# A two-layer mixture-of-experts kernel: blank slot rows written one expert at a time, pieces of 64 rows, and the short half of the down product on two halves of the array

## The reference, cut to what matters

```python
buf = zeros((E, C, D)).at[se, pos_c].add(where(valid, x[st], 0))      # E=64, C=384, D=256
g = einsum('ecd,efd->ecf', buf, w_gate)                                # F=176
u = einsum('ecd,efd->ecf', buf, w_up)
eo = einsum('ecf,edf->ecd', silu(g) * u, w_down)
gathered = eo[se, pos_c] * (sw * valid)[:, None]
y = zeros_like(x).at[st].add(gathered)
return y + shared_swiglu(hidden_states, sh_gate, sh_up, sh_down)
```

## Time and profile before

| | |
|---|---|
| runs | 615.86, 617.28, 621.86 us; median 617.28 |
| profiled execution | 624.11 us, of which the span is 622.4 us |
| mean granted TensorE clock | 0.937 of full |
| busy | PE 508.2, PEld 364.2, DVE 313.9, ACT 188.1, POOL 330.0 us |
| moved | 146.55 MB, 92394 packets |
| front | 0 to about 267.6 us; then the expert loop to about 596.1 us; then the last adds and the store |

### The profile page before, as it was taken

The page is one execution under the profiler, slowest core; times in us unless marked ns, Lnnn a source line. Parts: engine busy times, 40 slices in busy tenths (PEclk is TensorE's granted clock), DMA queues, the critical chain, the costliest instruction groups (busy, mean ns, idle before and its releaser), DMA issues.

```text
span 622.4 us, 11506 instructions
## 1 busy us (share of the span) xinstructions
PE 508.2 (82%) x2483; PEld 364.2 (59%) x2484; DVE 313.9 (50%) x823; ACT 188.1 (30%) x398; POOL 330.0 (53%) x289
## 2 busy tenths in 40 slices
PE   0797299489899899979999879999789898999920
PEld 0443153253545355558888757788668776889710
DVE  8731164274866862254445526555265544555424
ACT  0111012011221211033444425454255444455410
POOL 8900050572474767603767635655465545656750
PEclk9997689689999999989999979999799999999975
DMA  6999999996794222238999969999699989899779
GB/s 205 365 390 393 358 393 404 392 363 212 239 309 143 110 84 112 101 98 212 234 231 227 238 134 219 229 213 252 148 205 239 249 220 229 196 243 227 146 148 307
DMA packets 92394, 146.55 MB, mean 235 GB/s; under 512 B 10824, under 2 KB 72120, under 8 KB 92280
## 3 DMA queue, kind: packets, MB, share of 16 engines
q1 hardware_dynamic: 61608, 83.30, 42.6%
q0 software_dynamic: 30672, 61.75, 38.5%
HBM read 81.18 MB, written 63.83 MB: 233 GB/s over the span
## 4 chain that ended last, share of the span: by engine, by line
PE 49%; SPq 19%; DMA 10%; issue 10%; DVE 7%; POOL 3%; ACT 1%; POOLq 0%; DVEq 0%
PE bank L1074 21%; PE bank L1095 7%; PE bank L1096 7%; SPq L356 5%; SPq L355 5%; DMA x_g<-in_x 4%; PE bank L1055 4%; POOL slot_rows L491 3%; PE bank L935 2%; DMA wt<-in_wdt 2%; SPq L392 2%; PE bank L885 2%; SPq L363 2%; DVE M L749 1%; PE bank L956 1%
## 5 line engine op out<-in xcount | busy, mean ns | idle before, releaser
L502 POOL DMA_INDIRECT acc<-sil,sids x64 | 99.3, 1552 | 89.2 <-ACT sil L597 57.8
L491 POOL DMA_INDIRECT slot_rows<-ctok,sli x96 | 95.2, 991 | 80.0 <-issue 27.7
L502 POOL DMA_INDIRECT acc<-OH,sids x63 | 97.6, 1549 | 53.6 <-ACT OH L597 19.3
L1074 PE MATMUL bank<-xgT,wb 128*128 128x192 f32 (+9 forms) x384 | 85.2, 375 | 15.1 <-issue 12.8
L1074 PEld LDWEIGHTS bank<-xgT,wb 128*128 128x128 f32 (+1 forms) x384 | 65.6, 198 | 29.2 <-issue 17.0
L1096 PE MATMUL bank<-wt,hh 128*128 128x256 f32 x254 | 75.5, 379 | 0.0
L849 DVE TENSOR_TENSOR hh<-sg,bank 48x384 f32<-48x384 f32 x64 | 35.6, 556 | 74.0 <-ACT sg L586 73.2
L1096 PEld LDWEIGHTS bank<-wt,hh 128*128 128x128 f32 x254 | 48.3, 190 | 6.6
L584 ACT ACTIVATE sg<-bank 128x384 f32<-128x384 f32 x64 | 31.4, 491 | 55.4 <-PE bank L1074 55.1
L597 ACT ACTIVATE sil<-bank,wcol 128x256 f32<-128x256 f32 x64 | 29.7, 474 | 53.1 <-PE bank L1096 51.7
L597 ACT ACTIVATE OH<-bank,wcol 128x256 f32<-128x256 f32 x64 | 29.8, 474 | 51.3 <-PE bank L1096 50.0
(11 more groups left out here) (185 smaller groups left out, 739.1 us busy)
## 6 DMA issues: line engine op xcount, KB each, us to landing
cw<-slot_rows SPq DMA_DIRECT2D x127, 136.0 KB
cw<-in_cW SPq DMA_DIRECT2D x64, 256.0 KB, 6.2
wb<-in_wblk SPq DMA_DIRECT2D x32, 496.0 KB, 4.1
slot_rows<-xgT POOLq DMA_DIRECT2D x12, 1088.0 KB, 15.9
slot_rows<-wb POOLq DMA_DIRECT2D x12, 1088.0 KB, 25.0
h0T<-in_wblk SPq DMA_DIRECT2D x16, 496.0 KB
hT<-in_wblk SPq DMA_DIRECT2D x16, 496.0 KB
acc<-zrow POOLq DMA_DIRECT2D x2, 2432.0 KB
```

The lines of the kernel that those rows point to most:

```text
L491: pool.indirect_dma_start(slots_d, bass.IndirectOffsetOnAxis(sli[:, g % 2, k, t:t + 1], 0), ctok[:, g % 2, t, :], None, bounds_check=SLOTS ...
L502: pool.indirect_dma_start(acc[u % 2], bass.IndirectOffsetOnAxis(sids[:, u % SR, j:j + 1], 0), yo[u % UE][:, j, :], None, compute_op=ALU.ad ...
L1074: ins = mm(bank[o][0:m, 0:n], w(b, c), xgT[u % UE][:, c, 0:n], start=c == 0, stop=c == DC - 1)
```

## The change

1. **Blank rows.** The table is laid out expert by expert, 448 rows each (384 and 64 spare). POOL's 24 transfers, `s_init` and the two VectorE operations per group that made block numbers go. VectorE writes a fourth note, `UNUSED`, the first slot behind an expert's count. SP writes 64 blank rows from there (`fill`), for 12 experts ahead of the loop and then in step e for expert e+12; before it loads an expert's rows it waits for that write.
2. **Pieces.** `SIZE` counts thresholds of 64 rows. Row loads and `acc` scatters go in pieces of 128 or 64 rows, so that an expert's count is rounded up to 64. Each of three places in `by_pieces` is an If with an Else.
3. **Compact TensorE code.** `gate_up` runs on 192 or on 256 columns, and on columns 256 to 383 in a pass of its own ahead of it if the count is above 256. `down` and the transposes always do tiles 0 and 1.
4. **Down remainder.** `wt` is loaded twice, to partitions 0 to 47 and 64 to 111, the `hh` remainder of tile 1 is written to partitions 64 to 111, and L1096's product is on 48 rows: tiles 0 and 2 on array rows 0 to 47, tile 1 on rows 64 to 111.

```diff
-RB = 16
-SLOTS = E * CAP
+H = P // 2
+SPACED = CAP + H
+SLOTS = E * SPACED
+AHEAD = 5
-SIZES = [P, 3 * P // 2, 2 * P, 5 * P // 2, CAP]
+SIZES = [n * H for n in range(1, CAP // H + 1)]
...
-        def by_tiles(eng, size, work):
...
+        def by_pieces(eng, size, work):
+
+            with eng.If(size > 0):
+                work(0, P)
+            with eng.Else():
+                work(0, H)
+            for j in range(1, TJ):
+                with eng.If(size > 2 * j):
+                    work(j, P)
+                with eng.Else():
+                    with eng.If(size > 2 * j - 1):
+                        work(j, H)
+                    with eng.Else():
+                        eng.sem_inc(s_tick, 1)
...
             def weights(e, b):
...
                 sp.dma_start(wt[b][0:FT], wdt[bass.ds(e, 1), :, :].rearrange("a p n -> p (a n)")).then_inc(s_wb[b], 16)
+                sp.dma_start(wt[b][CU:CU + FT], wdt[bass.ds(e, 1), :, :].rearrange("a p n -> p (a n)")).then_inc(s_wb[b], 16)
...
+            sp.wait_ge(s_const, 3)
             sp.wait_ge(s_flags, 1)
+            get, start = notes(sp, 0)
+
+            def fill(e, u):
+                sp.dma_start(slots_d[bass.ds(get(UNUSED, e, u), H), :], blank[:, :]).then_inc(s_unused[u % UN], 16)
+
+            for e in range(UE + 3 + AHEAD):
+                fill(e, e)
             for q in range(2):
                 sp.wait_ge(s_scat[q], 16 * TOPK * TG * G // 2)
...
-                def load(j):
-                    sp.dma_start(xg[:, u % UE, j, :], blocks[bass.ds(e, 1), j * P // RB:(j + 1) * P // RB].rearrange("a b r c -> (a b) r c")).then_inc(s_xg[u % UE], 16)
+                def load(j, rows):
+                    sp.dma_start(xg[0:rows, u % UE, j, :], slots_d[bass.ds(e * SPACED + j * P, rows), :]).then_inc(s_xg[u % UE], 16)
 
                 size = get(SIZE, e, u)
...
+                sp.wait_ge(s_unused[u % UN], (16 // UN) * (e - u % UN + UN))
+                sp.sem_inc(s_tick, 1)
+                by_pieces(sp, size, load)
...
                 if not (isinstance(e, int) and e >= E - UE - 3):
+                    if not (isinstance(e, int) and e >= E - UE - 3 - AHEAD):
+                        fill(e + UE + 3 + AHEAD, u + UE + 3 + AHEAD)
                     rows_free(e + 3)
                     loads(e + UE + 3, u + UE + 3)
...
-            pool.wait_ge(s_w, 16 * 8)
-            for b in range(CAP // RB):
-                pool.dma_start(slots_d[b * E * RB:(b + 1) * E * RB, :].rearrange("(n p) c -> p n c", p=P),
-                               blanks[b % len(blanks)].unsqueeze(1).to_broadcast([P, E * RB // P, RW])).then_inc(s_init, 16)
...
-            pool.wait_ge(s_init, 16 * CAP // RB)
...
-                link(v.tensor_scalar(blk[:, :], blk[:, :], 1.5 * 2 ** 23, 1.5 * 2 ** 23, ALU.add, ALU.subtract))
-                link(v.scalar_tensor_tensor(sc[:, :], blk[:, :], float((E - 1) * RB), sc[:, :], ALU.mult, ALU.add))
...
-                v.tensor_tensor(hh[0:FT, u % 2, 1, :], sg[0:FT, 1, :], bank[4][CU:CU + FT, 0:CAP], ALU.mult).then_inc(s_hh, 1)
+                for lo, hi in ((0, P), (2 * P, CAP)):
+                    v.tensor_tensor(hh[0:FT, u % 2, 1, lo:hi], sg[0:FT, 1, lo:hi], bank[4][CU:CU + FT, lo:hi], ALU.mult)
+                v.tensor_tensor(hh[CU:CU + FT, u % 2, 1, P:2 * P], sg[0:FT, 1, P:2 * P], bank[4][CU:CU + FT, P:2 * P], ALU.mult).then_inc(s_hh, 1)
...
+                with pe.If(size > 3):
+                    gate_up(2 * P, CAP, False)
+                with pe.Else():
+                    pe.sem_inc(s_tick, 1)
+                with pe.If(size > 2):
+                    gate_up(0, 2 * P, True)
+                with pe.Else():
+                    gate_up(0, P + H, True)
...
+                def first(j):
+                    mm(bank[5 + j][:, 0:D], hh[:, u % 2, 0, j * P:(j + 1) * P], down_first(u % UE), start=True, stop=False)
+
+                def short(j):
+                    lo = (j % 2) * CU
+                    return mm(bank[5 + j][:, 0:D], hh[lo:lo + FT, u % 2, 1, j * P:(j + 1) * P], wt[u % UE][lo:lo + FT], start=False, stop=True)
...
+                with pe.If(size > 3):
+                    first(2)
+                    short(2)
                 with pe.Else():
...
+                    pe.sem_inc(s_tick, 1)
+                first(0)
+                first(1)
+                short(0).then_inc(s_dp, 1)
+                short(1).then_inc(s_dp, 1)
```

More of the change, by code:

```diff
@@ L91, in program @@
         zrow = sb("zrow", [P, D])
+        blank = sb("blank", [H, RW])
         i_q0 = sb("i_q0", [P, TT], I32)
@@ L223, in program @@
         s_ws = sem("shared_weights_loaded")
-        s_init = sem("slot_tokens_initialised")
+        s_unused = [sem(f"unused_slots_filled{i}") for i in range(UN)]
         s_x = sem("x_loaded")
@@ L1046, in tokens @@
             def tokens(e, u):
-                def work(tiles):
-                    pe.wait_ge(s_xg[u % UE], gathered)
-                    if u:
-                        pe.wait_ge(s_xs, e)
-                        pe.wait_ge(s_xv, e)
-                    for c in range(DC):
-                        for j in range(tiles):
-                            last = tr(bank[c][:, j * P:(j + 1) * P], xg[:, u % UE, j, c * P:(c + 1) * P], ident[:, :])
-                        last.then_inc(s_xp, 1)
-                gathered = get(GATHERED, e, u)
@@ L1059, in tokens, with turn @@
-                by_tiles(pe, get(SIZE, e, u), work)
+                def turn(c, j):
+                    return tr(bank[c][:, j * P:(j + 1) * P], xg[:, u % UE, j, c * P:(c + 1) * P], ident[:, :])
+                gathered = get(GATHERED, e, u)
+                size = get(SIZE, e, u)
+                pe.wait_ge(s_xg[u % UE], gathered)
+                if u:
+                    pe.wait_ge(s_xs, e)
+                    pe.wait_ge(s_xv, e)
+                pe.sem_inc(s_tick, 1)
+                with pe.If(size > 3):
+                    for c in range(DC):
+                        turn(c, 2)
@@ L1061, in step, with gate_up @@
+                with pe.Else():
+                    pe.sem_inc(s_tick, 1)
+                for c in range(DC):
+                    turn(c, 0)
+                    turn(c, 1).then_inc(s_xp, 1)
             def step(e, u, first=False):
                 b = u % UE
-                def gate_up(n):
-                    pe.wait_ge(s_wb[b], (32 // UE) * (e - b + UE))
-                    if isinstance(e, int) and e == E - 1:
-                        pe.wait_ge(s_xs, e + 1)
-                        pe.wait_ge(s_xv, e + 1)
-                    if not first:
-                        pe.wait_ge(s_hh, 2 * e)
+                def gate_up(lo, hi, told):
@@ L1077, in step @@
                 start(e, u)
-                by_rows(get(SIZE, e, u), gate_up)
+                size = get(SIZE, e, u)
+                pe.wait_ge(s_wb[b], (48 // UE) * (e - b + UE))
+                if isinstance(e, int) and e == E - 1:
+                    pe.wait_ge(s_xs, e + 1)
+                    pe.wait_ge(s_xv, e + 1)
+                if not first:
+                    pe.wait_ge(s_hh, 2 * e)
+                pe.sem_inc(s_tick, 1)
+                with pe.If(size > 3):
+                    gate_up(2 * P, CAP, False)
```

93 lines of the change are left out of this document (32 added, 61 removed).

## The result

| | median | range | runs |
|---|---|---|---|
| kernel before | 619.26 us | 615.86 to 621.86 | 4 |
| changed kernel | 670.24 us | 668.87 to 672.63 | 4 |

The ratio is 1.083, 95% interval 1.076 to 1.090: slower by 51 us, where 643 us (+26) was forecast. The profiled execution took 671.49 us, its span is 669.5 us; the forecast for it was 649.8.

The account below looks back on a forecast made before the run. Blank-row transfers cost the front 33.4 us; TensorE paced the loop, SP having 0.8 us a step to spare. With SP then setting the pace: 624.1 - 33.4 + 55 + 4 = 649.8, times 0.989 gives 643 us; range 586 to 675.

Parts of the forecast that it names:

- The front: Ahead of the loop: without the 24 blank-row transfers, late loads for TensorE come on time, -33.4 us (-28 to -36).
- The step of SP: In the loop: SP's added work makes its step 6.12 us, above the present 5.06, so SP sets the pace, +55 us.
- the second load (0.54): In SP's loop step: loading `wt` twice adds one more issue, 0.54 us a step.
- the fill (1.38): In SP's loop step: reading the note takes 0.84 us and issuing the blank-row write 0.54, together 1.38 us.
- the cheaper row issue (-0.6): In SP's loop step: row loads issue at 0.35 us instead of 0.657, about 0.6 us less a step.
- The wait for `s_unused` (0.2): In SP's loop step: waiting for the blank-row write, with its register and tick, adds 0.2 us (0.1 to 0.3).
- about four small steps more at 0.09, 0.35 us (0.15 to 0.5): In SP's loop step: extra compares, ticks and jumps of the 64-row pieces, 0.09 us each, add 0.35 us.
- SP's jumps back: In SP's loop: two jumps back, hidden before, now show at 2 us each, +4 us.
- TensorE's part: In the loop: compact code and down remainder add 13 us of TensorE work (-2 to +35), hidden under SP's longer step.
- An edit may add up to 0.8 us a step to SP for nothing: In the loop: SP's work of 4.25 us in a 5.06 us step leaves 0.8 us a step to spare.
- The rival with a hidden queue (586 us): In the loop: SP's added work stays within about 0.8 us a step, TensorE keeps the pace, 586 us; chance 0.22.
- Row issues do not get cheaper: In SP's loop step: row issues stay as dear as before, step 6.73 us, 674 us in all; chance 0.13.

Follow-up runs that it names:

- the kernel with whole tiles: Changed kernel, but SP loads whole 128-row tiles under two nested Ifs and blanks are 128 rows: 720.18 us (1.032 of before), measured again 625.37 us (1.003).
- the queue relieved: Changed kernel with loop fills issued by ScalarE, one `wt` load (48-row products not overlapping), whole 128-row tiles loaded by SP: 614.51 us, 0.991 of before.
- lazy rows of 128 on TensorE's old code: Kernel before with only the new table layout and blank rows of 128 per expert, written in the loop by ScalarE: 599.41 us, 0.967 of before.
- the kernel with pieces: Kernel before with blank rows of 64 issued in the loop by ScalarE, and `by_pieces` on SP and POOL; TensorE code old: 589.92 us, 0.946 of before.
- before + `wt` load + fill: Kernel before plus a second `wt` load and, in 52 steps, a note read and a 64-row write to a spare table, on SP: 693.31 us, 1.123.

## Why the prediction was right and wrong

- **The direction, the place and the mechanism were right.** SP's sequencer sets the pace, its waits vanish, TensorE waits for `wt` and `wb`; the run with SP's added work on the old TensorE code loses in the same way with nothing else changed.
- **The front** gave 31.0 us for 33.4: groups 1 and 2 took 37.97 us each instead of 36.54, the undisturbed pace.
- **The step of SP** was forecast at 6.12 us and was 6.54. The terms for the second load (0.54), the fill (1.38), and the cheaper row issue (-0.6) held to 0.07 us each. The wait for `s_unused` (0.2) was not to be seen, or the note read, now 0.276 us instead of 0.447, paid for it.
- **The step that failed is "about four small steps more at 0.09, 0.35 us (0.15 to 0.5)", the price of the pieces' branches.** It measured 0.9 us: 0.94 by the kernel with whole tiles, 0.89 by the table above. The error was to price a branch by its recorded duration, 45 ns, and as much again, though the earlier trace rows had the right price in them: between two row issues that one compare separates lie 0.29 us, of which the compare is 0.045. How the 0.9 us divide among compares, jumps, ticks and the gaps around them, no run separates.
- **SP's jumps back** were put at 2 us each. The two steps that hold them last 9.99 (349.50 to 359.49) and 9.7 us, some 3.5 us above their neighbours each: +7 for +4.
- Together: front +2.4, branches +0.55 us a step and the other terms -0.29, which is +13.5 in 52 steps (+14.8 by the mean of the steps without a jump), jumps +3, the end +1.2: 20 to 21.5 of the 21.7 us between 649.8 and the profiled 671.5.
- **TensorE's part was right and hidden.** The shape changes took 0.2 us, and the short products overlap. With the queue relieved, compact code and products without overlap cost 15 us where the terms give 19; POOL's pieces are in that figure.
- **"An edit may add up to 0.8 us a step to SP for nothing" was wrong**, though it did not enter the sum. The 5.06 us are a mean with two steps of 12 us in it; the other 50 have 0.52 us to spare, and with 0.54 us added TensorE waited 13.4 us for `wt` instead of 3.3.
- **The rival with a hidden queue (586 us)** was to be decided at an SP step of about 5.1 us; by the same reading it is about 4.8. The run with the queue relieved stands at 0.991, some 612 us of 617. It has 18 us that the rival hasn't (no overlap), and without the queue the prediction's terms give it 624.1 - 33.4 + 19 = 609.7, in the median 603 us. Most of what is missing is in the loop, which takes 0.3 us a step more with lazy rows of 128 on TensorE's old code already (16 us). With pieces of 64 this was not to be seen (5.07 us a step). Whether the changed kernel with pieces, overlap and a relieved queue would reach 586 us, no run shows.
- **"Row issues do not get cheaper"** (674 us) came within 4 us of the time for the wrong reason: the issues got cheaper as forecast.

The rule of the Trainium skill that the prediction weighed ("DMA: Bandwidth & Descriptors", "Why a DMA increments its semaphore by 16 and not by 1", how many engines a transfer runs on) agrees with the row issue's fall from 0.657 to 0.363 us, though no run here shows the engines of a transfer. It doesn't tell the other difference of these runs: the fill of 64 rows takes 0.494 us to issue and that of 128 rows 0.374, though 16 divides both. The drain at a change of mode, of which the Trainium skill speaks in "TensorEngine Tiling (Array Packing)", "Tiling Modes", agrees with the 0.2 us that the changes of shape take above.

## What to carry to other kernels

An engine that only issues transfers has a step time like any other: add up its issues, note reads, branches and jumps per step, take each price with the gap behind it and not from the instruction's own duration, and compare the sum with the loop's step before moving work to it. Take the slack from ordinary steps and not from the mean: two steps of 12 us made 0.52 us look like 0.8, and an issue of 0.54 us was not free. And when a change of several parts loses, try the parts alone: here the lazy rows and the pieces are worth 5.4% together, once the fill is issued by ScalarE and TensorE's code is left alone.

## What was not expected of the hardware

- Issuing a write of 64 rows of 1088 bytes to HBM costs SP more than one of 128 rows: 0.494 against 0.374 us by medians of 64 issues each, in the changed kernel and in that with whole tiles. ScalarE shows the same, 0.492 us in the kernel with pieces and 0.343 in that with lazy rows alone. The cause is open.
- The read of a note into a register takes SP 0.27 to 0.45 us by the median, by kernel, and the number of reads does not decide it: 0.447 with one a step (before) and 0.437 with two (before + `wt` load + fill), but 0.276 with two (changed) and 0.275 with one (pieces). The cause is open.
- An indirect scatter of up to 64 rows on POOL is hardly cheaper than one of 128: by the prediction's count at least 33 of 127 pieces are of 64 rows, and 33 scatters of the changed kernel took 1.42 to 1.44 us, all others 1.54 or more, as all 127 of the kernel before. That these 33 are those of 64 rows is inferred from the count.
